# Transposes of quantised weights on the DMA queue, the causal mask of the second score pass on GpSimd, and new orders, in a pre-norm decoder layer

## The chip, the cores and the metric
The kernel runs on one core of one Trainium2 chip. The time is the device time of one execution in microseconds (us), the median of the runs shown. All engines run their own program in order and meet only at semaphores: TensorE (PE, with its weight loads PEld), VectorE (DVE), ScalarE (ACT), GpSimd (POOL) and SyncE (SP), which issues nearly all DMAs.

## The reference
Eight sequences of 128 tokens, 256 features, all float32. Three residual blocks follow one another, each fed by a layer norm without weights:

```
q, k, v = x@Wq+bq, x@Wk+bk, x@Wv+bv      # 16 query heads and 4 key heads of 16 features, with rotary embedding
scores  = sum over the 4 query heads of each key head of q.k / sqrt(16), causal mask, softmax, times v
x = x + attention @ Wo + bo
x = x + cross attention of norm(x) over ctx (keys = values = ctx, masked by mask_BxS2_bk0)
x = x + ffn(norm(x)):  w1 (1408x256), w2 (256x704), x and h each quantised to 127 steps per row
        h = silu(gate) * up,  gate and up are the two halves of x_q @ w1_q^T;  out = h_q @ w2_q^T
```

The einsum of the scores sums over the query heads of a group, so the kernel sums Wq over them first. Quantised values are whole numbers from -127 to 127 times one scale per row of the weight.

## The kernel before, in words
The host only lays the inputs out. Everything is loaded into SBUF at the start by SP, in the order of use: first weights, x, context, w1 in three parts, w2, the context again. One sequence (batch j, 0 to 7) fills the 128 partitions with its tokens. The work of a batch is a chain of small steps, and the chains of the eight batches are interleaved by lists of calls written out for each engine (PE from L560, ACT from L759, DVE from L1050, POOL from L1203). A step stands at its place in its engine's list and waits there for its semaphores, so what stands behind a late step is late too.

The steps of a batch:
- Self attention. project (PE) gives q, k and v; rotate (DVE), rotate_c (POOL) and rotate_sum (DVE) apply the rotary table; transpose_qk (PE) and evacuate_qk (ACT) give q and k by feature. The scores are computed twice. First pass: mask_scores writes the causal mask (-1e30) into PSUM with a matmul of the identity, scores adds q.k, and max_scores (DVE) takes each query's maximum. It goes into a spare column of q; transpose_q_max (PE) and evacuate_q_max (ACT) transpose that. Second pass, with keys on the partitions: mask_keys writes the transposed mask causal_T (4 matmuls a batch, L339), score_keys adds k.q minus the maximum, exp_self (ACT, L625) gives the probabilities p_self_T, 128 keys by 4 heads by 128 queries, already transposed. weigh_values (PE, L364, L367) multiplies them with v and with ones, for the sums. invert_sums, normalise_y (DVE), project_out (PE), residual_1 (DVE).
- Cross attention. square_1 (ACT) and rstd_2 (POOL, L1149, L1151) give the norm's scale; transpose_x1, cross_scores, max_cross, bias_cross, exp_cross, transpose_cross_p, readout (PE), residual_2 (DVE). The context is centred by centre_ctx (POOL) with means from mean_ctx (PE, L290: 16 products of 60 equal columns each, a matmul instruction twice for float32; one column is used).
- Feed forward. amax_x, step_x, invert_x (DVE), quantise_x (ACT), transpose_x_int (PE), evacuate_x_int (ACT); gate_product and up_product (PE, L456), where the gate weights are split in two parts, gate_hi (rounded by the write as float32r) and gate_lo (the rest); tanh_gate and finish_gate, or silu_gate; widen_gate (POOL, L1169) multiplies the gate by the row of up scales; hidden (DVE, L1021), amax_h, quantise_h, transpose_h, evacuate_h, down (PE, L538), scale_down (DVE), add_residual (POOL). Two buffers each hold the gate and the hidden values, so hidden(1) has to be done before up_product(2). The last batch is split in halves to shorten its chain.

Weights of the feed forward: amax_w1, scale_w1, invert_w1 (DVE) and quantise_w1 (ACT) give w1_int, int16, with output features on the partitions. They have to be transposed:
- gate: rescale_gate (POOL, L1157) multiplies by the scale, transpose_gate (PE, L408) transposes in float32 four blocks at a time into bank ps_r, upper_gate (ACT) and lower_gate (DVE, L951) take the two parts out of it;
- up: transpose_up (PE, L419) transposes whole numbers as 16-bit patterns, evacuate_up (ACT) converts; spread_up_scale (PE, L429) spreads the scales over the partitions, evacuate_up_scale (ACT) copies them to up_row;
- w2: transpose_w2 (PE, L439, and L441 for the scale), evacuate_w2 (DVE).

Filler matmuls (keep_warm, L263) stand where TensorE would wait at the start. GpSimd also makes the masks and zeroes buffers at the start, and rstd_1 (L1108) computes the first norm's scales, the last six batches in one call.

Of the kernel before, what the change touches and what calls it, by code (L numbers as in the profile page):

```python
# [32 lines left out]
def decoder_layer(nc, w_first_in, x_zero_in, x_first_in, x_second_in, wo_in, mask_in, x_in, xT_in, ctxT_in, ctx_in, w1_in, w2_in, out):  # L33
    P, B, DC, T = ctxT_in.shape
    D = DC * P
    H = N_KV
# [12 lines left out]
    GT = -(-FF // P)  # L49
    CM = 61  # L50
# [6 lines left out]
    with ExitStack() as stack:  # L57
# [7 lines left out]
        causal_T = sb("causal_T", [P, T], BF16)  # L65
# [28 lines left out]
        w1_q = sb("w1_q", [P, GT, D])  # L94
# [3 lines left out]
        up_row = sb("up_row", [P, FF])  # L98
# [4 lines left out]
        w2_int = sb("w2_int", [P, DC, FF], I16)  # L103
        w2_T = sb("w2_T", [P, FC, D], BF16)
# [61 lines left out]

        def x_token(j):
            return x_second[:, 0:D] if j == 1 else x_aug[:, j, 0:D]

        def x_feature(j, c):  # L170
# [16 lines left out]
            warm_ready causal_T_zero causal_T_ready wq_summed w_mean_done wqkv_c_ready bias_half_summed bias_summed bias_copied b_cos_done b_sin_done b_rope_ready  # L187
# [5 lines left out]
            scores_done negmax_done q_max_transposed q_max_T_ready keys_done p_T_ready  # L193
# [6 lines left out]
            w1_amax_done w1_scale_done w1_inv_ready w1_int_ready w1_q_ready w1_transposed gate_hi_ready gate_lo_ready  # L200
            up_transposed up_int_ready up_scale_spread up_row_ready
            w2_amax_done w2_scale_done w2_inv_ready w2_int_ready w2_transposed w2_ready
# [32 lines left out]
        def _(sp):  # L235
# [20 lines left out]
        def _(pe):  # L256
# [3 lines left out]
            def keep_warm(n):  # L260

                for _ in range(n):
                    nc.tensor.matmul(ps_r[:, 0:2 * T], warm[:, 0:P], warm[:, :], start=True, stop=True)  # L263
# [17 lines left out]
            def mean_ctx(last, k):  # L281
# [6 lines left out]
                for j in range(B):  # L288
# [47 lines left out]
            def mask_keys(j, heads):  # L336

                for h in heads:
                    nc.tensor.matmul(ps_s[:, h, 0:T], ident_b[:, :], causal_T[:, :], start=True, stop=False)  # L339

            def mask_other_keys(j):
                if j == 0:
                    done(pe, "causal_T_ready", 0)
                done(pe, "negmax_done", j)
                mask_keys(j, range(1, H))

            def score_keys(j):

                done(pe, "q_max_T_ready", j)
                mask_keys(j, range(1))  # L350
                for h in range(H):
                    nc.tensor.matmul(ps_s[:, h, 0:T], qk_T[j % 3][h * HP:(h + 1) * HP, 1, :],  # L352
                                     q_max_T[j % 3][h * HP:(h + 1) * HP, :], start=False, stop=True).then_inc(s["keys_done"], 1)

            def weigh_values(j):
# [6 lines left out]
                done(pe, "p_T_ready", j)  # L362
# [38 lines left out]
            def transpose_gate(p, last, k):  # L401
                bank_r_free(pe, last, k)
                if p == 0:
                    done(pe, "ident_ready", 0)
                done(pe, "w1_q_ready", p)
                for i in range(2):
                    for c in range(DC):
                        last = nc.tensor.transpose(ps_r[:, (2 * i + c) * P:(2 * i + c + 1) * P],  # L408
                                                   w1_q[:, 2 * p + i, c * P:(c + 1) * P], ident[:, :])
                last.then_inc(s["w1_transposed"], 1)  # L410

            def transpose_up(p, last, k):
# [859 lines left out]
```

## Time and profile before

| | us |
|---|---|
| median of 3 runs | 101.81 (101.38 to 102.7) |
| profiled execution | 102.22 |
| its span, first to last instruction | 100.4 |
| TensorE busy | 92.1 (92%) |
| VectorE busy | 75.4 (75%) |
| ScalarE busy | 65.1 (65%) |
| GpSimd busy | 61.5 (61%) |
| mean granted TensorE clock | 0.988 |

Busy times overlap; the shares are of the span. In the profile the matmul time of TensorE overlaps that of its neighbours, since matmuls are pipelined: the mean duration of one matmul is longer than what it adds. The chain of waits shows what each adds. A float32 matmul shows as two instructions. A clock of 1.00 is 2.4 GHz, 0.5 is 1.2 GHz.

### The profile page before, as it was taken

The page shows a single profiled execution, that of the slowest core. Times are in us where ns is not written, and L with a number is a line of the kernel's source. Part 1 is how long each engine was busy: PE and PEld are TensorE (multiplying, and loading weights), DVE is VectorE, ACT ScalarE, POOL GpSimd, SP SyncE. Part 2 cuts the span into 40 slices and gives each one's busy share as a digit, 9 for nine tenths or more (in the row PEclk, how much of TensorE's full clock was granted, in tenths as well). Part 3 has the DMA queues.
Part 4 walks back from the last instruction along what each step waited for, and adds up shares of the span by engine and source line. Part 5 has one row for each costly group of instructions (what it writes and reads, how often), then busy time and mean ns, then how long its engine had stood idle before and what let it go on. Part 6 is the DMA issues. An engine that isn't in the chain of part 4 may idle for free.

```text
span 100.4 us, 2487 instructions
## 1 busy us (share of the span) xinstructions
PE 92.1 (92%) x834; PEld 71.3 (71%) x834; DVE 75.4 (75%) x217; ACT 65.1 (65%) x175; POOL 61.5 (61%) x130
## 2 busy tenths in 40 slices
PE   5999699989999999999999999998999999999560
PEld 4788479766867787867877797776887977775220
DVE  5135979828999998697696669797878696998731
ACT  1403210489978677777787879689777897988420
POOL 5476666179922755976188674882489992872220
PEclk9999999999999999999999999999999999999995
DMA  2999999930000000000000000000000010021121
GB/s 35 368 342 421 416 407 415 351 98 3 0 7 3 0 3 0 7 0 0 7 0 0 0 0 7 3 0 0 0 0 0 7 52 3 0 104 52 52 104 52
DMA packets 4521, 8.34 MB, mean 83 GB/s; under 512 B 349, under 2 KB 3358, under 8 KB 4382
## 3 DMA queue, kind: packets, MB, share of 16 engines
q1 hardware_dynamic: 4272, 7.96, 21.6%
q10 hardware_dynamic: 238, 0.23, 0.7%
q8 instruction: 6, 0.10, 0.5%
q14 instruction: 5, 0.04, 0.1%
HBM read 7.15 MB, written 1.05 MB: 82 GB/s over the span
## 4 chain that ended last, share of the span: by engine, by line
PE 72%; DVE 13%; POOL 6%; issue 3%; ACT 3%; DVEq 0%; ACTq 0%; POOLq 0%
PE ps_s L456 11%; PE ps_r L263 8%; PE ps_q L304 6%; PE ps_y L538 4%; PE ps_r L290 4%; PE ps_y L372 3%; POOL gate_up L1169 3%; PE ps_r L399 3%; PE ps_s L352 3%; PE ps_s L328 3%; PE ps_x L388 2%; PE ps_q L312 2%; PE ps_y L364 2%; PE ps_s L339 2%; PE ps_s L482 2%
## 5 line engine op out<-in xcount | busy, mean ns | idle before, releaser
L1169 POOL TENSOR_TENSOR gate_up<-gate,up_row 128x704 f32<-128x704 f32 x7 | 11.9, 1699 | 6.6 <-ACT gate L738 5.0
L263 PE MATMUL ps_r<-warm 128*128 128x256 bf16 x58 | 9.5, 330 | 1.0 <-DVE warm L786 1.0
L1144 POOL TENSOR_TENSOR rot_c<-rot,b_rope 128x128 f32<-128x128 f32 x8 | 3.6, 456 | 9.1 <-DVE rot L861 9.1
L263 PEld LDWEIGHTS ps_r<-warm 128*128 128x128 bf16 x58 | 6.7, 120 | 3.1 <-DVE warm L786 1.0
L456 PE MATMUL ps_s<-gate_hi,x_int_T 128*128 128x352 f32 x28 | 7.7, 355 | 0.0
L884 DVE RECIPROCAL y_rsum<-ps_y 128x128 f32<-128x128 f32 x8 | 7.6, 950 | 0.1
L1200 POOL TENSOR_TENSOR y_out<-ffn,x_aug 128x256 f32<-128x256 f32 x7 | 4.8, 690 | 4.4 <-DVE ffn L1040 4.4
L538 PE MATMUL ps_y<-w_T,h_T 128*128 128x256 bf16 (+1 forms) x42 | 6.5, 275 | 0.9 <-DVE ffn L1040 0.8
L456 PE MATMUL ps_s<-up_int,x_int_T 128*128 128x352 f32 x32 | 6.8, 335 | 0.1
L456 PE MATMUL ps_s<-gate_lo,x_int_T 128*128 128x352 f32 x28 | 6.8, 323 | 0.0
L749 ACT ACTIVATE h_int<-hid,h_inv 128x704 int16<-128x704 f32 x7 | 6.1, 877 | 0.3 <-DVE h_inv L1035 0.3
L1026 DVE TENSOR_REDUCE h_amax<-hid 128x1 f32<-128x704 f32 x7 | 6.1, 877 | 0.1
L861 DVE TENSOR_TENSOR rot<-ps_q,rope_r 128x256 f32<-128x256 f32 x8 | 3.4, 422 | 3.7 <-PE ps_q L304 3.6
L620 ACT COPY q_max_T<-ps_s 128x128 f32<-128x128 f32 x8 | 2.1, 265 | 6.2 <-PE ps_s L334 5.9
L1021 DVE SCALAR_TENSOR_TENSOR hid<-ps_s,x_scale,gate_up 128x704 f32<-128x704 f32 x5 | 4.8, 951 | 1.8 <-PE ps_s L456 1.2
L538 PEld LDWEIGHTS ps_y<-w_T,h_T 128*128 128x128 bf16 (+1 forms) x42 | 3.6, 97 | 3.3 <-issue 1.5
L738 ACT ACTIVATE gate<-ps_s,x_scale 128x704 f32<-128x704 f32 x5 | 4.2, 847 | 2.3 <-PE ps_s L456 2.3
L879 DVE TENSOR_REDUCE qk_rot<-ps_s 128x4 f32<-128x512 f32 x8 | 5.5, 685 | 0.3
L304 PE MATMUL ps_q<-wqkv_c,xT 128*128 128x192 f32 x24 | 5.3, 341 | 0.5 <-ACT qk_T L614 0.5
L625 ACT ACTIVATE p_self_T<-ps_s 128x512 f32<-128x512 f32 x8 | 4.8, 596 | 1.4 <-PE ps_s L352 1.3
L1175 POOL TENSOR_SCALAR ctx_aug<-ctx_aug,valid_mean,ctx_negmean 128x256 f32<-128x256 f32 x8 | 4.4, 549 | 1.7 <-DVE ctx_negmean L853 1.7
L456 PEld LDWEIGHTS ps_s<-up_int,x_int_T 128*128 128x128 f32 x32 | 5.2, 189 | 0.2 <-DVE hid L1021 0.2
(197 smaller groups left out, 290.6 us busy)
## 6 DMA issues: line engine op xcount, KB each, us to landing
ctxT<-in_ctxT SPq DMA_DIRECT2D x1, 1024.0 KB, 8.7
w_raw<-in_w SPq DMA_DIRECT2D x2, 512.0 KB, 11.2
ctx_aug<-in_ctx SPq DMA_DIRECT2D x1, 1024.0 KB, 17.1
out_x<-y_out SPq DMA_DIRECT2D x8, 128.0 KB, 1.7
x_aug<-in_x SPq DMA_DIRECT2D x1, 768.0 KB, 7.0
xT<-in_xT SPq DMA_DIRECT2D x1, 768.0 KB, 9.9
w_raw<-in_w SPq DMA_DIRECT2D x1, 704.0 KB, 14.8
x_first<-in_x_first SPq DMA_DIRECT2D x1, 416.0 KB, 4.5
```

The lines of the kernel that those rows point to most:

```text
L263: nc.tensor.matmul(ps_r[:, 0:2 * T], warm[:, 0:P], warm[:, :], start=True, stop=True)
L304: last = nc.tensor.matmul(ps_q[:, 0:6 * QK], x_feature(j, c), wqkv_c[:, c, :, :], start=c == 0, stop=c == DC - 1)
L456: last = nc.tensor.matmul(ps_s[:, first + i, 0:FH], x_int_T[:, j, c, :], w[:, c, i * FH:(i + 1) * FH], start=c == 0 and w is parts[0], sto ...
L538: last = nc.tensor.matmul(ps_y[:, 0:D], h_T[j % 2][0:n, f, :], w2_T[0:n, f, :], start=f == 0, stop=f == FC - 1)
L625: nc.scalar.activation(p_self_T[j % 3][:, :, :], ps_s[:, :, 0:T], ACT.Exp).then_inc(s["p_T_ready"], 1)
L749: nc.scalar.mul(h_int[j % 2][:, :], hid[j % 2][:, :, :].rearrange("p i f -> p (i f)"), h_inv[:, j:j + 1]).then_inc(s["h_int_ready"], 1)
L879: nc.vector.tensor_reduce(qk_rot[j % 3][:, 0, :, DH], ps_s[:, :, 0:T], AX.X, ALU.max, negate=True).then_inc(s["negmax_done"], 1)
L884: nc.vector.reciprocal(y_rsum[j % 3][:, :], ps_ys).then_inc(s["y_rsum_done"], 1)
L1021: nc.vector.scalar_tensor_tensor(hid[j % 2][:, :, :], ps_s[:, 2:4, 0:FH], scale, gate_up[j % 2][:, :, :], ALU.mult, ALU.mult).then_inc(s[" ...
L1026: nc.vector.tensor_reduce(h_amax[:, j:j + 1], hid[j % 2][:, :, :].rearrange("p i f -> p (i f)"), AX.X, ALU.max, apply_absolute_value=True) ...
L1169: nc.gpsimd.tensor_tensor(gate_up[j % 2][:, :, :], gate[j % 2][:, :, :], up_row[:, :].rearrange("p (i f) -> p i f", i=2), ALU.mult).then_i ...
L1200: nc.gpsimd.tensor_tensor(y_out[:, j, :], ffn[j % 3][:, :], x_aug[:, j, 0:D], ALU.add).then_inc(s["y_out_ready"], 1)
```

## The change
- The second mask on TensorE (causal_T, mask_keys, mask_other_keys) is gone. score_keys starts its PSUM groups itself, exp_self exponentiates later keys too, and a new GpSimd step, drop_later_keys, sets those probabilities to 0 before weigh_values.
- w1_int is transposed by two DMA transposes on SP's queue into w1_T, with gate's 6 row blocks first, then up's 5. The scales of w1 are stored to DRAM element by element and loaded back as a row on every partition, w1_row, of which up_row is a part. Both reuse the memory of w1_raw.
- scale_gate (GpSimd) converts w1_T to float32 and multiplies with the row; upper_gate and lower_gate work on 704 columns per half, from SBUF. evacuate_up (ACT) reads w1_T.
- w2_int is converted to bf16 by widen_w2 (GpSimd), transposed by two more DMA transposes; its scale goes through DRAM as well.
- TensorE loses transpose_gate, transpose_up, spread_up_scale, transpose_w2 and the 7 fillers after scores(0). mean_ctx uses 8 columns instead of 60 and is split; its second half stands behind scores(1). mask_scores(0) moves behind transpose_qk(0).
- All four lists have new orders.

```diff
+            done(sp, "w1_scale_done", len(W1_PARTS) - 1)
+            sp.dma_start(w1_row_dram.rearrange("(o p) -> p o", p=P), w1_scale[:, :], allow_slow_non_contiguous=True).then_inc(s["w1_row_stored"], 16)
+            done(sp, "w1_int_ready", 2)
+            sp.dma_start_transpose(w1_T[:, 0:GT + 1, :, :].rearrange("p o c t -> p (o c) t"),
+                                   w1_int[:, 0:GT + 1, :].rearrange("p o d -> p (o d)")).then_inc(s["gate_T_loaded"], 16)
+            done(sp, "w1_int_ready", 4)
+            sp.dma_start_transpose(w1_T[:, GT + 1:WT, :, :].rearrange("p o c t -> p (o c) t"),
+                                   w1_int[:, GT + 1:WT, :].rearrange("p o d -> p (o d)")).then_inc(s["up_T_loaded"], 16)
+            sp.wait_ge(s["w1_row_stored"], 16)
+            sp.dma_start(w1_row[:, :], w1_row_dram.unsqueeze(0).to_broadcast([P, 2 * FF])).then_inc(s["w1_row_loaded"], 16)
+            done(sp, "w2_scale_done", 0)
+            sp.dma_start(w2_row_dram.rearrange("(c p) -> p c", p=P), w2_scale[:, :], allow_slow_non_contiguous=True).then_inc(s["w2_row_stored"], 16)
+            sp.wait_ge(s["w2_row_stored"], 16)
+            sp.dma_start(w2_row[:, :], w2_row_dram.unsqueeze(0).to_broadcast([P, D])).then_inc(s["w2_row_loaded"], 16)
+            for c in range(DC):
+                done(sp, "w2_bf_ready", c)
+                sp.dma_start_transpose(w2_T[:, :, c * P:(c + 1) * P], w2_bf[:, c, :]).then_inc(s[f"w2_T_{c}_loaded"], 16)
...
             def score_keys(j):
                 done(pe, "q_max_T_ready", j)
-                mask_keys(j, range(1))
                 for h in range(H):
                     nc.tensor.matmul(ps_s[:, h, 0:T], qk_T[j % 3][h * HP:(h + 1) * HP, 1, :],
-                                     q_max_T[j % 3][h * HP:(h + 1) * HP, :], start=False, stop=True).then_inc(s["keys_done"], 1)
+                                     q_max_T[j % 3][h * HP:(h + 1) * HP, :], start=True, stop=True).then_inc(s["keys_done"], 1)
...
+            def upper_gate(c):
+                done(act, "gate_T_ready", c)
+                nc.scalar.copy(gate_hi[:, c, :], gate_T[:, c, :]).then_inc(s["gate_hi_ready"], 1)
+            def evacuate_up(c):
+                act.wait_ge(s["gate_T_loaded"], 16)
+                act.wait_ge(s["up_T_loaded"], 16)
+                nc.scalar.copy(up_int[:, c, 0:FL], w1_T[:, GT, c, FL:P])
+                nc.scalar.copy(up_int[:, c, FL:FF].rearrange("p (o t) -> p o t", t=P), w1_T[:, GT + 1:WT, c, :]).then_inc(s["up_int_ready"], 1)
...
+            def lower_gate(c):
+                done(dve, "gate_T_ready", c)
+                done(dve, "gate_hi_ready", c)
+                nc.vector.tensor_tensor(gate_lo[:, c, :], gate_T[:, c, :], gate_hi[:, c, :].bitcast(F32), ALU.subtract).then_inc(s["gate_lo_ready"], 1)
...
+            def drop_later_keys(j):
+                done(pool, "p_T_ready", j)
+                nc.gpsimd.affine_select(out=p_self_T[j % 3][:, :, :], in_=p_self_T[j % 3][:, :, :], compare_op=ALU.is_ge, fill=0.0, base=0,
+                                        pattern=[[0, H], [1, T]], channel_multiplier=-1).then_inc(s["p_causal_ready"], 1)
+            def scale_gate(c):
+                done(pool, "w1_int_ready", 4)
+                pool.wait_ge(s["gate_T_loaded"], 16)
+                pool.wait_ge(s["w1_row_loaded"], 16)
+                nc.gpsimd.tensor_copy(gate_T[:, c, 0:GT * P].rearrange("p (o t) -> p o t", t=P), w1_T[:, 0:GT, c, :])
+                nc.gpsimd.tensor_copy(gate_T[:, c, GT * P:FF], w1_T[:, GT, c, 0:FL]).then_inc(s["gate_T_widened"], 1)
+                done(pool, "gate_T_widened", c)
+                nc.gpsimd.tensor_tensor(gate_T[:, c, :], gate_T[:, c, :], w1_row[:, 0:FF], ALU.mult).then_inc(s["gate_T_ready"], 1)
+            def widen_w2(c):
+                done(pool, "w2_int_ready", c)
+                if c == 0:
+                    done(pool, "w2_bf_zero", 0)
+                nc.gpsimd.tensor_copy(w2_bf[:, c, 0:FF], w2_int[:, c, :]).then_inc(s["w2_bf_ready"], 1)
...
 # GpSimd's list
+            rstd_1(0, 1, 1); scale_rope(0); sum_bias(); rope_bias(); rotate_c(0); rstd_1(1, 2, 2); centre_x(0)
+            scale_rope(1); rotate_c(1); centre_x(1); rstd_1(2, B, 3); drop_later_keys(0); scale_rope(2)
+            centre_x(2); centre_x(3); scale_rope(3); rotate_c(2); centre_x(4); centre_x(5); scale_rope(4)
+            centre_x(6); scale_rope(5); centre_x(7); centre_ctx(0); drop_later_keys(1); scale_rope(6)
+            rotate_c(3); rstd_2(0); centre_ctx(1); widen_w2(0); centre_ctx(2); drop_later_keys(2); rotate_c(4)
+            scale_gate(0); rstd_2(1); drop_later_keys(3); centre_ctx(3); rotate_c(5); rstd_2(2); scale_gate(1)
+            drop_later_keys(4); scale_rope(7); rotate_c(6); centre_ctx(4); whole_x2(0); rstd_2(3); centre_ctx(5)
+            scale_x(0); drop_later_keys(5); whole_x2(1); rotate_c(7); widen_w2(1); rstd_2(4); centre_ctx(6)
+            drop_later_keys(6); scale_x(1); whole_x2(2); centre_ctx(7); rstd_2(5); drop_later_keys(7)
+            whole_x2(3); scale_x(2); whole_x2(4); rstd_2(6); widen_gate(0); scale_x(3); whole_x2(5); rstd_2(7)
+            scale_x(4); widen_gate(1); whole_x2(6); scale_x(5); widen_gate(2); widen_gate(3); scale_x(6)
...
 # ScalarE's list, its part around the new waits
+            quantise_w1(3); evacuate_q_max(1); evacuate_qk(2); exp_self(1); square_1(0); quantise_w1(4)
+            evacuate_x1(0); scale_v(3); quantise_w2(0); evacuate_q_max(2); evacuate_qk(3); exp_cross(0)
+            exp_self(2); evacuate_cross_p(0); evacuate_up(0); quantise_w2(1); scale_v(4); evacuate_x1(1)
+            evacuate_up(1); evacuate_q_max(3); evacuate_qk(4); square_1(1); exp_self(3); upper_gate(0)
...
 # VectorE's list, its part around the w1 scales
+            rotate_sum(1); amax_w1(0); scale_w1(0); invert_w1(0); amax_w1(1); scale_w1(1); invert_w1(1)
+            rotate(2); invert_sums(0); max_scores(1); normalise_y(0); rotate_sum(2)
+            amax_w1(2); scale_w1(2); invert_w1(2); keep_valid(); residual_1(0); negate_ctx_mean(); rotate(3)
...
 # TensorE's list, its parts around the first batches and the last cross attention
+            keep_warm(11, ps_x); transpose_qk(0); mask_scores(0); project(1); scores(0); mean_ctx(None, 0)
+            transpose_q_max(0); transpose_qk(1); score_keys(0); project(2); mask_scores(1); weigh_values(0)
+            scores(1); mean_ctx_half(1); transpose_q_max(1); project_out(0); transpose_qk(2); score_keys(1)
...
+            gate_product(2); transpose_cross_p(7); readout(7, "x2_ready", 6); up_product(1)
+            transpose_x_int(4, "x2_ready", 7); gate_product(3); transpose_x_int(5, "x_int_T_ready", 4)
+            up_product(2); transpose_h(0); gate_product(4); down(0); transpose_h(1)
```

## Rows read from the trace of the kernel before

**Rows 1.** Windows: stretch, its length, busy us (instructions) of PE, PEld, DVE, ACT, POOL; clock; DMA share; GB/s.

```profile
25.00:30.00 5.00, 4.62 (x56) 3.60 (x56) 4.64 (x10) 4.26 (x13) 3.12 (x8) 1.00 0.02 3
30.00:35.00 5.00, 4.97 (x59) 3.84 (x60) 4.69 (x15) 3.76 (x12) 2.56 (x6) 1.00 0.00 2
...
50.00:55.00 5.00, 5.00 (x65) 3.86 (x63) 3.67 (x11) 3.83 (x13) 4.08 (x12) 1.00 0.00 0
```

**Rows 2.** Chain of waits in order of time: start us, us, engine, tile, line.

```profile
66.04 1.67 POOL gate_up L1169
...
68.94 0.91 DVE hid L1021
...
91.96 0.57 DVE hid L993
```

**Rows 3.** Chain of waits, TensorE's pieces that the change touches and their neighbours.

```profile
7.29 0.39 PE ps_x L273 x4
...
14.01 0.87 PE ps_r L263 x7
...
15.20 3.71 PE ps_r L290 x32
...
21.80 0.45 PE ps_r L408 x4
...
34.76 0.17 PE ps_s L339 x3
...
48.98 0.67 PE ps_r L429 x6
...
57.09 0.45 PE ps_r L419 x6
...
70.80 0.47 PE ps_r L439 x6
71.27 0.42 PE ps_r L441 x2
```

**Rows 4.** Groups by line and form, VectorE: busy us, mean ns, idle before.

```profile
L951 DVE TENSOR_TENSOR gate_lo<-ps_r,gate_hi 128x256 fp32r<-128x256 f32 x5 | 1.9, 417 | 0.6 <-ACT gate_hi L666 0.6
L986 DVE TENSOR_TENSOR gate_up<-gate,up_row 128x352 f32<-128x352 f32 x2 | 1.4, 749 | 0.0
```

**Rows 5.** GpSimd: one window (POOL is the fifth busy time), its start, three groups.

```profile
17.60:67.70 50.10, 48.68 (x529) 38.04 (x529) 40.57 (x111) 38.85 (x121) 32.76 (x73) 1.00 0.08 24
16.22 1.34 POOL L1108 TENSOR_TENSOR r<-ln_var,pow_exp 128x6 f32<-128x6 f32 x1
L1157 POOL TENSOR_SCALAR w_q<-w_int,w_scale 128x256 f32<-128x256 int16 x6 | 2.8, 483 | 2.7 <-ACT w_int L657 2.7
L1149 POOL TENSOR_SCALAR ln_var<-x_sumsq 128x1 f32<-128x1 f32 x8 | 1.5, 191 | 1.4 <-ACT y_out L630 0.9
L1089 POOL TENSOR_SCALAR_AFFINE_SELECT causal<-causal 128x128 bf16<-128x128 bf16 x1 | 0.3, 292 | 0.1
```

**Rows 6.** Chain of waits, batch 3: its second scores, its weigh_values.

```profile
40.56 0.43 PE ps_s L352 x8
...
43.85 0.40 PE ps_y L364 x8
```

**Rows 7.** DMA: a queue with packets, MB, share; issues with KB, us to landing.

```profile
q10 hardware_dynamic: 238, 0.23, 0.7%
...
ctx_aug<-in_ctx SPq DMA_DIRECT2D x1, 1024.0 KB, 17.1
out_x<-y_out SPq DMA_DIRECT2D x8, 128.0 KB, 1.7
...
w_first<-in_w_first SPq DMA_DIRECT2D x1, 384.0 KB, 3.7
```

**Rows 8.** Window from hid(1) to the last hidden, columns as in rows 1.

```profile
68.90:92.00 23.10, 22.82 (x163) 17.56 (x161) 19.47 (x49) 19.19 (x38) 14.96 (x20) 1.00 0.07 24
```

**Rows 9.** Window at the end of the span, columns as in rows 1.

```profile
98.00:100.40 2.40, 0.00 (x0) 0.00 (x0) 0.34 (x1) 0.00 (x0) 0.00 (x0) 0.51 0.16 55
```

More of the change, by code:

```diff
@@ L287, in mean_ctx, with mean_ctx_half @@
                 pe.wait_ge(s["ctxT_loaded"], 16)
-                for j in range(B):
+                mean_ctx_half(0)
+            def mean_ctx_half(half):
+                means = ps_r[:, 0:B * CM].rearrange("p (b n) -> p b n", n=CM)
+                for j in range(half * B // 2, (half + 1) * B // 2):
                     for c in range(DC):
@@ L586, in _ @@
-            up_product(1); readout(6, "x_int_T_ready", 4); transpose_cross_p(7); up_product(2)
-            transpose_w2(0, "x2_ready", 6); gate_product(3); transpose_w2(1, "w2_ready", 0); transpose_h(0)
-            gate_product(4); up_product(3); transpose_x_int(5, "w2_ready", 1); down(0); transpose_h(1)
-            readout(7, "x_int_T_ready", 5); gate_product(5); up_product(4); transpose_x_int(6, "x2_ready", 7)
-            down(1); transpose_h(2); gate_product(6); up_product(5); down(2); transpose_h(3)
@@ new lines, in _ @@
+            scores(1); mean_ctx_half(1); transpose_q_max(1); project_out(0); transpose_qk(2); score_keys(1)
+            project(3); transpose_x1(0); mask_scores(2); scores(2); weigh_values(1); cross_scores(0)
+            transpose_q_max(2); transpose_qk(3); score_keys(2); project(4); transpose_cross_p(0); project_out(1)
+            readout(0, "valid_ready", 0); mask_scores(3); transpose_x1(1); scores(3); weigh_values(2)
+            transpose_qk(4); transpose_q_max(3); cross_scores(1); score_keys(3); project(5); project_out(2)
@@ new lines, in _ @@
+            mask_scores(4); scores(4); transpose_cross_p(1); weigh_values(3); transpose_q_max(4)
+            readout(1, "x2_ready", 0); transpose_x1(2); transpose_qk(5); score_keys(4); cross_scores(2)
+            project(6); mask_scores(5); project_out(3); scores(5); transpose_cross_p(2)
+            transpose_x_int(0, "x2_ready", 1); weigh_values(4); transpose_x1(3); transpose_q_max(5)
+            readout(2, "x_int_T_ready", 0); cross_scores(3); transpose_qk(6); score_keys(5); project(7)
+            project_out(4); transpose_x_int(1, "x2_ready", 2); mask_scores(6); transpose_cross_p(3); scores(6)
@@ new lines, in _ @@
+            transpose_x1(4); weigh_values(5); transpose_q_max(6); readout(3, "x_int_T_ready", 1); score_keys(6)
+            cross_scores(4); transpose_qk(7); mask_scores(7); project_out(5); scores(7)
+            transpose_x_int(2, "x2_ready", 3); transpose_cross_p(4); weigh_values(6); transpose_q_max(7)
+            transpose_x1(5); readout(4, "x_int_T_ready", 2); score_keys(7); cross_scores(5); project_out(6)
+            gate_product(0); transpose_cross_p(5); weigh_values(7); transpose_x_int(3, "x2_ready", 4)
@@ new lines, in _ @@
+            transpose_x1(6); up_product(0); cross_scores(6); readout(5, "x_int_T_ready", 3); gate_product(1)
+            project_out(7); transpose_cross_p(6); transpose_x1(7); readout(6, "x2_ready", 5); cross_scores(7)
+            gate_product(2); transpose_cross_p(7); readout(7, "x2_ready", 6); up_product(1)
+            transpose_x_int(4, "x2_ready", 7); gate_product(3); transpose_x_int(5, "x_int_T_ready", 4)
+            up_product(2); transpose_h(0); gate_product(4); down(0); transpose_h(1)
@@ L596, in _ @@
+            transpose_x_int(6, "x_int_T_ready", 5); up_product(3); gate_product(5); up_product(4); down(1)
+            transpose_h(2); gate_product(6); up_product(5); transpose_x_int(7, "x_int_T_ready", 6)
+            transpose_h(3); down(2); up_product(6); last_gate(0); transpose_h(4); last_gate(1); down(3)
+            transpose_h(5); up_product(7); down(4); transpose_h(6); down(5); down(6); last_transpose_h_a()
+            last_transpose_h_b(); last_down_a(); last_down_b()
         @block.scalar
```

265 lines of the change are left out of this document (69 added, 196 removed).

## The prediction
> **What bounds the kernel now.** I read the windows of 5 us first [rows 1]. TensorE is busy 4.6 to 5.0 of every 5 us from 25 to 90 us, always at its upper clock (granted 1.00), and VectorE is close behind (4.6 to 4.7 of 5 between 25 and 35). So between 30 and 60 us TensorE's own work sets the pace. GpSimd has 0.9 to 2.4 us of idle in those 5. The chain of waits [rows 2] says the same with one exception: from 60 to 69 us it runs through GpSimd: the first two gate products times the scale row (L1169, 1.7 us each) with small pieces between, then VectorE's hid(1) at 68.94; the rows are the second L1169 and the two ends. From there TensorE again, to a tail from 91.96 in which one batch passes serially through all engines. Two places matter here: the end of the second L1169, 67.7 us (call it T), and the 32.7 us from T to the end of the span. The profiled execution took 102.2 us at a span of 100.4; the median is 101.8, so a span converts to a median by +1.4.
>
> **TensorE.** It loses the second causal mask, 32 matmuls at 0.17 per 3: 1.8 us; 3 groups of gate transposes at 0.45: 1.35; 2 of up transposes at 0.45: 0.9; 2 spreads of the up scale at 0.67: 1.34; the w2 groups, 2 x (0.47 + 0.42): 1.78; 7 filler matmuls: 0.87 [rows 3]. Sum 8.0 us, of which 1.8 lie behind T. The context means are cut from 60 columns to 8, but 32 matmuls of 60 columns take 0.116 us each while those of 64 columns take 0.098 and the f32 transposes of 128 columns 0.11 [rows 3]: the weights set that price, so I take 0 (bounds: 0, and 52/60 of 3.71, 3.2 us). Half of them are put behind the second scores. With the fillers gone, the first q_max transpose comes at about 15.9 instead of 18.9. That is latency, not work: it lets the first exp go earlier, and the half comes back.
>
> **VectorE and ScalarE.** VectorE loses five lower_gate pieces of 0.42 and one of 0.28 (2.4), and evacuate_w2, 1.9. It gains two subtractions of 704 columns with both operands in SBUF. The nearest rows are L986, 0.75 us for 352 columns, so 1.5 each at most, and L951, 0.42 for 256 with one operand in PSUM, so 1.1 [rows 4]. I take 1.3 each; net -1.7, and the bounds move it by 0.4. ScalarE's copies of gate, up and up scale go from 4.4 to about 3.8. Neither moves the end; the cover is that both have idle beside TensorE and GpSimd, and if it were gone they would cost nothing new, since both lose work.
>
> **GpSimd.** This is where the bill falls. Before, it is busy 32.76 us between 17.6 (its 6-batch pow ends, L1108) and T [rows 5]. Out: 6 rescales at 0.48, 2.8 us. In: 8 selects of 512 columns. The selects of 128 columns took 0.29; a one-input op of 1 column (L1149) takes 0.19 and one of 256 (L1157) 0.48 [rows 5], so 0.6 if most of 0.29 is overhead, 1.17 if none is; nearer to the first, since every one-input row shows overhead: 0.7, 5.6 us in sum. In: twice a copy of 640 and one of 64 columns (0.92 and 0.27 on the line through those two rows) and a product of 704, the shape of L1169, 1.7 [rows 2]: 5.8. In: two w2 copies of 704, 1.0 each: 2.0. And rstd_2(7) is now ahead of T: 0.74. That is 44.1 us of work, and about 30 dependent pairs with the 0.1 us that the chain shows as issue, 2.8. T can't be before 17.6 + 44.1 + 2.8 = 64.5 us. The new memset for w2 (0.6 to 1.4 by the other memsets) and the causal_T pair it replaces lie in GpSimd's idle before 5.4 us: 0.
>
> The GPSIMD Engine Reference of the Trainium skill (section 3.1) puts a two-input operation on GpSimd at about twice VectorE's time; here L1169 [rows 2] takes 1.7 against the 1.5 that 704 columns would be in two halves of L986 [rows 4], only 1.13 times. By the page the two products of scale_gate would rather be 3.0 each, an estimate, and T 2.6 later.
>
> The select also adds a link: exp, then select, then weigh_values. Before, TensorE ran 2 to 3 us of other work between the last score matmul and weigh_values (batch 3: 40.99 to 43.85 [rows 6]), and exp uses 0.8 of it. 0.8 more fits, if GpSimd comes to it in time. It is in order: behind a wait for a DMA, all selects are late, then TensorE.
>
> **The new DMA train on SP's queue.** Each step of it, in order: store of w1_scale (1408 single elements), transposes of gate and of up, row load of 704 KB to 128 partitions, then w2's. All SP loads were issued by 5.9 us, the last landed at 23, and SP's output stores start after 80, so nothing else is hurt. Start: VectorE's third amax_w1 is now behind max_scores(1), about 22.8 us. Prices [rows 7]: ACT's small-packet queue moved 238 packets in 0.7% of 16 engines x 100.4 us, 47 ns each, so 1408 packets over 16 engines are 4.1 us, and +1.4 for a landing (a 128 KB store lands in 1.7). Row load: 704 KB at 0.4 MB/us, 3.2. Transposes: no row shows one. Below, a plain 384 KB load, 3.7. Above, the slowest landing, 17.1. If each 128-element piece is a packet, gate has 1536 (4.5 us) and up 1280 (3.8). I take 2.5 us of queue time each, nearer to the plain load, since the bytes are the same. The store's packets are then through at 27, the transposes at 29.5 and 32, the row at 32 + 1.8 of data, and it lands at about 34.5. By packets alone (4.5 and 3.8) it is 39; by the lowest prices, with the store as quick as a 128 KB one, below 30.
>
> Waiters: scale_gate(0) on GpSimd, reached at 30.3 (12.3 us of work from 17.6, plus small waits), with rstd_2(1), drop_later_keys(3) and rotate_c(5) behind it; evacuate_up(0) on ScalarE behind evacuate_cross_p(0), about 29, with quantise_w2(1), scale_v(4) and q_max(3) behind it. The row at 34.5 is a wait of 4.2; I charge 3 us of it and T = 67.5, since GpSimd would have waited about 1 us for rotations anyway. w2's train needs its row and blocks only at down(0), after 75: 0.
>
> The DMA page of the Trainium skill (DMA: Bandwidth & Descriptors, Latency and other measured facts) gives 261 GB/s for a DMA transpose, which would be an estimate of 1.5 us for gate's 393 KB and would make the train some 3 us shorter. No row here can show it. Its rule that a non-contiguous last dim lowers to one descriptor per element (section Rules for kernel authors) is what the 1408 packets would be.
>
> **Behind T.** From 68.9 to 92.0 all engines have 19 to 23 us in 23 [rows 8]. TensorE leaves 1.78 (w2), and gate_product(3) 1.53, readout(7) 0.63 and one x_int transpose 0.13 now stand ahead: 4.1. VectorE leaves 2.0 of w2 and about 1.7 of two residuals with their maxima. ScalarE has 19.2 and drops under 1, so it is next: the stretch becomes about 19. Gain 4. The tail from the last hidden is the same work: 8.4 us.
>
> **Sum.** 100.4 + (67.5 - 67.7) - 4 = 96.2 of span, +1.4: 97.6 us.
>
> **Rivals.**
>
> A. The train is in time (transposes near the plain load): T falls to GpSimd's 64.5, a span of 93.2, 94.6 us; a little more if selects cost 0.6. TensorE agrees: up_product(1) ends at 68.7 before, less 6.3 removed, plus 1.2 moved ahead, 63.6. For: all queues are empty then. Against: two engines arrive at their waits around 30.
>
> B. The train goes at packet prices: row at 39, a stall of 8.7, T = 73.2: 103.3; 102 where GpSimd's other waits absorb part. For: the 47 ns rest on small packets as these are. Against: they are from plain loads. No difference that can be measured (2% is 2.0 us, what a measurement of this kernel tells from no change).
>
> C. Slower. The transposes take as long as the slowest load or longer, one after the other. Break-even: T + 32.7 - 4 + 1.4 = 101.8 gives T = 71.7, a stall of 7.2, the row at 37.5. Two transposes at 17.1 and the row land at 27 + 17 + 17 + 3 = 64: T = 98, 128 us. At 8 each it is about 46, T = 80, 110 us. It decides from 40 us on for the row: 104 us. For: the trace has landings of 10 to 17 us. Against: those stood in a full queue, and this one is empty.
>
> D. The clock. With fillers gone and TensorE waiting near 30 us, the granted clock could fall to 1.2 GHz. The trace shows a mean of 0.51 in the last 2.4 us, in which TensorE has no matmul [rows 9], and 1.00 in all stretches before the tail. 3 to 6 us of TensorE work at half the clock add 3 to 5 us to the forecast: 101 to 103. "TensorE: Matmul & The Clock Gate" of the Trainium skill (Part 1) says that idleness brings the throttle; the row agrees in kind.
>
> **Chances.** Forecast (95.5 to 99.8) 0.38; A 0.20; B 0.18; C 0.18; D 0.06. Faster by over 2% (below 99.8): forecast and A, 0.58, less 0.01 for its upper edge. Within 2%: most of B and D, 0.22. Slower: C and B's edge, 0.21. Range: 93.5 (A with cheap selects) to 103.5 (B's end), with C and a little of A left out, about 2 in 10.
>
> **What would show it.** Right: SP's transposes land 3 to 5 us after issue, GpSimd idle of 2 to 5 us ahead of gate_T's first copy, selects at 0.7, the second L1169 ending at 66 to 69, TensorE about 84 busy, hid(1) to the last hidden 19. Wrong: transposes over 8 us (C), no wait at gate_T (A), a PEclk below 9 around 30 us (D), or selects over 1 us, which add 3 us to T.

## The result and the profile after

The changed kernel takes 106.19 us (median of 4 runs, 105.43 to 106.27) against 102.25 of the kernel before on the same chip: ratio 1.040 (95% interval 1.029 to 1.050), slower. The forecast was 97.6 with a range to 103.5, so it was wrong in sign and in size. The profiled execution took 106.22 us at a span of 104.4. Here and below, ratios and intervals compare only each kernel's fast runs, those within 1.5% of its quickest, while a median with its spread is of all runs, and where a single run is fast no interval stands.

The windows answer to [rows 1]; columns as there:

```profile
15.00:20.00 5.00, 4.86 (x47) 3.81 (x49) 4.09 (x12) 3.33 (x9) 3.81 (x8) 0.66 1.03 384
...
30.00:35.00 5.00, 3.28 (x39) 2.18 (x37) 3.13 (x10) 0.84 (x3) 1.28 (x3) 1.00 1.29 42
35.00:40.00 5.00, 1.56 (x8) 1.53 (x8) 0.93 (x4) 3.48 (x10) 0.51 (x1) 0.67 0.64 185
40.00:45.00 5.00, 5.00 (x45) 3.65 (x44) 1.86 (x5) 3.22 (x11) 4.58 (x9) 0.65 0.04 2
```

Between 30 and 40 us, where TensorE used to be full, it has 4.8 us of work in 10, and then it is full at a clock of 0.65. The waits from 24 to 46 us (who waited <- for whom: sum, times, longest) name the releaser:

```profile
POOL w_raw L1101 <- DMA w_raw<-w_row_dram: 7.7, 1, 7.7
ACT up_int L637 <- DMA w_T<-w_int: 5.4, 1, 5.4
PEld ps_q L339 <- issue: 5.4, 1, 5.4
PE ps_q L339 <- ACT v_pad L576: 5.2, 1, 5.2
```

GpSimd stands at scale_gate(0) for the row, ScalarE at evacuate_up(0) for the transpose of up, and TensorE waits for the scale_v that stands behind that in ScalarE's list. The row lands at about 39.4 us. From 39.5 to the end of the second gate_up product GpSimd then never waits longer than 0.2 us, so the row sets that end. The DMA issues (KB, us to landing) answer to [rows 7]:

```profile
w_raw<-w_row_dram SPq DMA_DIRECT2D x1, 704.0 KB, 4.6
...
w_T<-w_int SPq DMA_TRANSPOSE x2, 10.7
w_row_dram<-w_scale SPq DMA_DIRECT2D x1, 5.5 KB, 11.1
w_row_dram<-w_scale SPq DMA_DIRECT2D x1, 1.0 KB, 10.4
```

The smallest transfers are the slowest: 5.5 KB in 11.1 us, 1 KB in 10.4. The point T, the end of the second gate_up product, and VectorE's hid(1) and last hidden answer to [rows 2] (timeline: start, us, engine, line):

```profile
73.31 1.69 POOL L1122 TENSOR_TENSOR gate_up<-gate,w_raw 128x704 f32<-128x704 f32 x1
75.69 0.94 DVE L960 SCALAR_TENSOR_TENSOR hid<-ps_s,x_square,gate_up 128x704 f32<-128x704 f32 x1
...
95.91 0.57 DVE L932 SCALAR_TENSOR_TENSOR hid<-ps_s,x_scale,gate_up 128x352 f32<-128x352 f32 x1
```

T is 75.0 instead of 67.7. From T to the end it is 29.4 us, before 32.7. So all of the loss, and more, stands ahead of T: 7.3 us later, and 3.3 of them back behind it.

### The profile page after: what moved, and what is told of

Same layout as the page of the kernel before. It is cut to its first block, busy times and chain, and to the rows that moved or that the text cites. A ratio compares the mean times of both kernels' runs of the same rounds, so it can differ in the third digit from the quotient of the medians.

```text
span 104.4 us, 2307 instructions
## 1 busy us (share of the span) xinstructions
PE 89.2 (85%) x743; PEld 67.6 (65%) x743; DVE 73.6 (71%) x207; ACT 64.5 (62%) x172; POOL 72.7 (70%) x139
## 4 chain that ended last, share of the span: by engine, by line
PE 58%; ACT 10%; DMA 10%; DVE 8%; POOL 6%; issue 5%; DVEq 0%; ACTq 0%; POOLq 0%
PE ps_s L429 13%; DMA w_T<-w_int 10%; PE ps_r L285 7%; PE ps_q L331 5%; PE ps_r L317 4%; PE ps_s L367 3%; PE ps_y L511 3%; PE ps_x L403 3%; PE ps_y L387 2%; PE ps_s L355 2%; PE ps_y L379 2%; POOL ctx_aug L1128 2%; PE ps_q L478 2%; PE ps_q L339 1%; PE ps_x L478 1%
## 5 line engine op out<-in xcount | busy, mean ns | idle before, releaser
L1122 POOL TENSOR_TENSOR gate_up<-gate,w_raw 128x704 f32<-128x704 f32 x7 | 11.9, 1700 | 2.3 <-ACT gate L689 2.3
L339 PE MATMUL ps_q<-ident,qk_rot 128*128 128x128 f32 x16 | 3.4, 300 | 5.6 <-ACT v_pad L576 5.2
L285 PE MATMUL ps_r<-warm 128*128 128x256 bf16 x40 | 7.2, 356 | 1.1 <-DVE warm L737 1.1
L331 PE MATMUL ps_q<-wqkv_c,xT 128*128 128x192 f32 x24 | 7.6, 456 | 0.6 <-ACT qk_T L582 0.6
L285 PEld LDWEIGHTS ps_r<-warm 128*128 128x128 bf16 x40 | 5.0, 130 | 2.8 <-DVE warm L737 1.1
L1101 POOL CAST w_raw<-w_T 128x640 f32<-128x640 int16 x2 | 1.4, 719 | 7.7 <-DMA w_raw<-w_row_dram 7.7
L331 PEld LDWEIGHTS ps_q<-wqkv_c,xT 128*128 128x128 f32 x24 | 5.3, 257 | 1.6 <-ACT qk_T L582 1.1
L339 PEld LDWEIGHTS ps_q<-ident,qk_rot 128*128 128x128 f32 x16 | 2.0, 149 | 6.2 <-issue 5.4
L1086 POOL TENSOR_SCALAR_AFFINE_SELECT p_self_T<-p_self_T 128x512 f32<-128x512 f32 x8 | 5.1, 644 | 1.2 <-ACT p_self_T L593 0.8
L403 PE MATMUL ps_x<-ctxT,x1c_T 128*128 128x128 f32 x32 | 5.8, 308 | 0.0
```

Of the source, the lines that this page charges most:

```text
L285: nc.tensor.matmul(bank[:, 0:2 * T], warm[:, 0:P], warm[:, :], start=True, stop=True)
L331: last = nc.tensor.matmul(ps_q[:, 0:6 * QK], x_feature(j, c), wqkv_c[:, c, :, :], start=c == 0, stop=c == DC - 1)
L339: last = nc.tensor.transpose(ps_q[:, QT0 + i * T:QT0 + (i + 1) * T], qk_rot[j % 3][:, i], ident[:, :])
L403: last = nc.tensor.matmul(ps_c, x1c_T[j % 3][:, c, :], ctxT[:, j, c, :], start=False, stop=c == DC - 1)
L1086: nc.gpsimd.affine_select(out=p_self_T[j % 3][:, :, :], in_=p_self_T[j % 3][:, :, :], compare_op=ALU.is_ge, fill=0.0, base=0, pattern=[[0, ...
L1122: nc.gpsimd.tensor_tensor(gate_up[j % 2][:, :, :], gate[j % 2][:, :, :], up_row[:, :].rearrange("p (i f) -> p i f", i=2), ALU.mult).then_i ...
```

## The experiments

All ratios are to the kernel before, timed on the same chip; a difference between two variants is often one between two chips. An element store is one that writes every scale as a transfer of its own, 4 bytes long. The code cuts are shortened.

**e1_probe.** The whole train on the queue of the kernel before, one transfer after the other, results unused:

```diff
+ sp: store w1_scale by elements; wait; transpose gate; wait; transpose up; wait; load row; wait;
+     store w2_scale by elements; wait; store w1_scale, 64 bytes apart; wait; store it as 128 lines; wait
```

> The kernel before, with seven DMAs more on SP's queue between 28 us and the output stores, each issued only when the one before has landed, so each is alone: store of the w1 scales as 1408 single elements, transpose of gate's 6 row blocks, of up's 5, row load of 704 KB, store of the w2 scales as 256 single elements, a store of the w1 scales with 64 bytes between elements, and one in 128 runs of 44 bytes. Nothing uses their results. Theory S (the element stores are slow in themselves, the transposes quick): first store 9 us or more alone, w2's too, transposes at 5 us or less, time 102. Rival T (the transposes are slow and held the stores up, which shared the engines with them): first store 5.5 us, w2's under 3, transposes 8 to 10 us alone. Either way the time stays within 1% of before, since SP has nothing else to do.

Measured: 106.38 us, ratio 1.041 (1.033 to 1.049), though nothing waits for any of it. SP's own waits show what each costs alone:

```profile
SPq L258 <- DMA w_row_dram<-w_scale: 10.4, 1, 10.4
SPq L269 <- DMA w_row_dram<-w_scale: 7.2, 1, 7.2
SPq L271 <- DMA pad_dram<-w_scale: 3.4, 1, 3.4
SPq L267 <- DMA w_raw<-w_row_dram: 3.2, 1, 3.2
SPq L261 <- DMA w_raw<-w_int: 2.9, 1, 2.9
```

The element stores take 10.4 and 7.2 us in an empty queue; the same 1408 elements 64 bytes apart take 3.4 and gate's transpose 2.9 beyond its issue (3.9 from issue to landing, the median of both). So the transposes are quick and the store is slow by itself. That the time rose by 4 us was foreseen by no theory.

**e2_warm.** The changed kernel with the seven fillers after scores(0) and 60 columns in mean_ctx again.

```diff
- scores(0); mean_ctx(None, 0)        - CM = 9
+ scores(0); keep_warm(7); mean_ctx(None, 0)        + CM = 61
```

> The changed kernel with the 7 fillers behind scores(0) again and 60 columns in the context means. Theory (the early falls of the clock are off the path, since ScalarE and GpSimd wait for DMAs whose start hangs on VectorE): clock at 1.00 from 10 to 33 us, but TensorE then waits longer ahead of 38 us, the long idle and the second fall stay: 105 to 106.5. Rival (the early clock costs what it takes): 3 us less, 103.

Measured: 107.04, ratio 1.046 (1.037 to 1.055). No gain: the clock is at 1.00 from 15 to 35 us now, but the waits for the transfers take up what it gives (ScalarE stands 6.7 us for up's transpose instead of 5.4).

**e3_later.** The changed kernel with evacuate_up and upper_gate (ACT), lower_gate (DVE) and scale_gate (POOL) some steps later in their lists.

> The changed kernel with scale_gate, evacuate_up, upper_gate and lower_gate some batches later in the lists of GpSimd, ScalarE and VectorE, so that their DMAs have landed; nothing else. Theory (the wait of 5.2 us of TensorE and the 7.3 us at 1.2 GHz behind it are the loss): both go, 106.2 - 5.2 - 3.6 = 97.4, with 96.5 to 99.5 as GpSimd paces the second half. Rival (GpSimd's added work is the loss and the wait only hides it): 103 or more.

Measured: 104.61, ratio 1.024 (1.016 to 1.033). The two DMA waits are gone, but only 1.6 us of the 106.2 with them. The element stores are still there, and in the profiled execution, the longest of the four, GpSimd waits elsewhere, for a sum of squares of ScalarE that is late itself:

```profile
36.29 0.19 POOL L1092 TENSOR_SCALAR ln_var<-x_sumsq 128x1 f32<-128x1 f32 x1 [4.51 <-ACT y_out L598]
...
40.99 0.60 ACT L593 ACTIVATE p_self_T<-ps_s 128x512 f32<-128x512 f32 x1 [0.17 <-PE ps_s L367]
...
41.66 0.64 POOL L1086 TENSOR_SCALAR_AFFINE_SELECT p_self_T<-p_self_T 128x512 f32<-128x512 f32 x1 [2.06 <-issue]
```

The last idle is marked "issue", which reads as if nothing were waited for. It is a wait for data all the same: the select needs the probabilities of ScalarE's line above, which end at 41.59. So this run says only that the loss doesn't hang on those two waits alone.

**e4_select.** The select alone: the kernel before with the 32 mask matmuls replaced by 8 selects on GpSimd.

> The kernel before with the second mask's 32 matmuls replaced by the 8 selects on GpSimd, nothing else of the change. Theory: TensorE loses 1.8 us, GpSimd gains 8 x 0.64 = 5.1; the link of 0.7 us fits between exp and weigh_values: 100.5 to 102. Rival: the selects stand late in GpSimd's list and hold TensorE: 104.

Measured: 102.87, ratio 1.010 (1.006 to 1.014). TensorE is busy 90.5 us instead of 92.1 and idle for as much more: the work is gone, the time is not. Whether the link or the 5.1 us more on GpSimd costs it, no run separates.

**e5_store and e6_moves.** The kernel before with one part of the train each: w1's element store alone, or everything of w1 but with the scales stored as lines.

```diff
e5: + sp.dma_start(w1_row_dram "(o p) -> p o", w1_scale)        # 1408 elements
e6: + sp.dma_start(w1_row_dram "(p o) -> p o", w1_scale)        # 128 lines of 44 bytes
e6: + both transposes, row load
```

> The kernel before with one transfer more: SP's queue stores w1_scale (128 x 11) to a row in DRAM element by element, as the changed kernel does, once it is complete (about 24 us). Nothing waits for it. Theory H (the store of single 4-byte elements keeps the DMA engines busy for some 10 us, and the next block of each engine's instructions, which the same DMA engines bring, comes late; engines then stand still until the store is through): most of the 4.2 us that all seven transfers together cost comes back, 104.5 to 106.5, with an instruction packet of 2 to 3.5 us instead of 0.4, and two or three engines idle to the moment at which the store lands. Rival M (it is the volume: two transposes and the 704 KB row load compete with the kernel's work): the store alone costs nothing, 101.8 to 102.6.

> The kernel before with all the bulk transfers of w1 on SP's queue, their results unused: both transposes (gate and up), the 704 KB load of a row to all partitions, and the scale stored as 128 lines of 44 bytes in place of 1408 single elements. Theory H: 101.8 to 102.8, no engine waits for instructions. Rival M: 104.5 to 106.5, and e5 costs nothing.

Measured: e5 105.48 (102.95 to 107.66) beside 102.47 of the kernel before; e6 102.23, ratio 1.000 (0.996 to 1.005). 1.4 MB of transposes and row cost nothing, 5.5 KB in single elements 0.5 to 5 us. Late beside the store are the packets that bring the engines their own instructions; the DMA view counts them on the same 16 DMA engines. In the kernel before, such a packet around 24 us (window of 1 us; packets, MB, share of 16 engines):

```profile
q14 instruction: 1, 0.01, 3.6%
```

In e5, windows 25 to 26 and 27 to 28:

```profile
q14 instruction: 1, 0.01, 20.8%
...
q8 instruction: 1, 0.02, 17.7%
```

20.8% of 16 engines over 1 us is 3.3 us for one packet, where it was 0.6. It ends about 28.8, and there two engines go on, out of idles that no data explain:

```profile
28.77 0.37 ACT L672 CAST gate_hi<-ps_r 128x256 fp32r<-128x256 f32 x1 [1.13 <-remote]
28.81 0.42 DVE L865 TENSOR_TENSOR rot<-ps_q,rope_r 128x256 f32<-128x256 f32 x1 [0.56 <-remote]
```

The changed kernel has two of them, at 32 (1.9 us) and at 42 (2.9 us). But e1 shows that the packet can't be all of it. Its long packet, 3.4 us, is over at 33.1, and the longest idles end 4 us later, just before the store lands at 37.8:

```profile
37.44 0.96 DVE L911 RECIPROCAL y_rsum<-ps_y 128x128 f32<-128x128 f32 x1 [3.65 <-remote]
37.57 0.27 ACT L647 COPY q_max_T<-ps_s 128x128 f32<-128x128 f32 x1 [4.07 <-remote]
```

So the engines stand still while an element store is under way; by what they are held isn't shown.

**e7_line and e8_line_warm.** The changed kernel with both scale rows stored in lines of 512 bytes; e8 has e2's edit as well.

```diff
- sp.dma_start(w1_row_dram "(o p) -> p o", w1_scale)
+ pe:  transpose(ps_r[0:11, 384:512], w1_scale, ident)
+ act: copy(scale_line[0:11], ps_r[0:11, 384:512])
+ sp.dma_start(w1_row_dram "(o p) -> o p", scale_line[0:11])      # between the two transposes
  (w2's two columns in the same way)
```

> The changed kernel, with both scale rows stored as whole lines: TensorE transposes w1_scale (128 x 11) and w2_scale (128 x 2) into a free part of PSUM, ScalarE copies them out (one short copy each), and SP stores 11 (2) lines of 512 bytes; the rest as it was. Theory H: store in 1.5 us, transposes landed by 32, row by 33; the 5.4 us wait of ScalarE and the 7.7 us wait of GpSimd shrink to under 2 together; the second gate_up product ends near 69 instead of 75.0; 99 to 101.5. Rival M: the transposes stay near 10 us, 104 or more. Rival C (the clock falls at 16 and 23 us, and what it takes from the attention stages sets the end once the waits are gone): the waits go, the second product ends at 71 to 73, 101.5 to 104.

> The kernel of e7 and with it what e2 put back: seven 256-column fillers after the first scores and 60 columns in place of 8 in each product of the mean of ctx. Theory H alone: as e7 within 0.5. Rival C: 1 to 3 us less than e7, with a granted clock of 1.00 to the end of the attention stages, and perhaps less than the kernel before.

Measured: e7 99.72, ratio 0.977 (0.971 to 0.982); e8 99.60, ratio 0.973 (0.966 to 0.981). Both beat the kernel before. e7's transfers:

```profile
w_raw<-w_row_dram SPq DMA_DIRECT2D x1, 704.0 KB, 4.3
...
w_T<-w_int SPq DMA_TRANSPOSE x2, 3.8
```

The same transposes land in 3.8 us instead of 10.7, GpSimd's wait for the row is 1.2 instead of 7.7, ScalarE's for up's transpose is gone, and T is 68.4:

```profile
66.70 1.68 POOL L1143 TENSOR_TENSOR gate_up<-gate,w_raw 128x704 f32<-128x704 f32 x1
```

**e9_store3 and e10_padded3.** The kernel before with three stores of the same 1408 elements in turn, to neighbouring places or 64 bytes apart.

> The kernel before with the element store of e5 three times, one after the other (each waits for the one ahead), from 24 us on; nothing else waits for them. It doubles and trebles the suspected cost: e5 alone ran from 102.95 to 107.66. Theory H (blocks of instructions come late while such a store is under way): the stores hold the DMA engines for about 31 us, three or four blocks fall into that, 106 to 114 and less spread relative to the cost. Rival M (the four microseconds of e5 are chance, or belong to the clock): 102 to 104.

> As e9, three stores of the same 1408 elements of 4 bytes, but each element to a place of its own 64 bytes from the next. The number of packets and of bytes is that of e9. Theory H with neighbours as the cause of the slow store: 3.8 us each, no instruction packet much over 1 us, 102 to 103.5. Rival N (the number of small packets is what delays instructions, wherever they go): as e9 in proportion to the time that the stores take, a third of its excess or more, 104 to 106.

Measured: e9 112.28 (106.91 to 113.5); e10 102.36, ratio 1.002 (0.997 to 1.007). With as many packets and bytes, only the neighbours cost: 10 us by the median and 4.7 in the quickest run, against nothing. Four instruction packets take 3.4, 2.8, 3.2 and 3.9 us in e9; in e10 none takes over 1.2.

**e11_line_warm_masks.** e8 with the select undone: the mask by 32 matmuls again.

> The kernel of e8 with the select undone: the causal mask of the second score pass added on TensorE by 32 matmuls as in the kernel before, the 8 selects of GpSimd gone. In e8 GpSimd is busy 4.4 to 4.8 of each 5 us from 35 to 60 us. Theory G (GpSimd sets the time of the attention stages there, its 8 selects of 0.65 us with it): 97 to 99. Rival P (TensorE takes back 3.5 us of mask matmuls and is the bound again): 100 to 102. Neither: 99.2 to 100.

Measured: 98.62 (98.12 to 98.97), ratio 0.965 (0.959 to 0.971), the quickest of all. The select is worth minus 1.0 us here (e8 and e11 ran on different chips, and their intervals overlap), minus 0.7 in e4.

**e12, e13, e15, e16.** One of the two rows stored by elements again, in e7 (e12, e13) and in e8 (e15, e16).

> The kernel of e7 with one thing back as in the changed kernel: the 256 scales of w2 are stored element by element. Theory H: the store takes 7 to 10 us from about 33 us and w2's transposes follow late, which nothing waits for; an instruction block that falls into it comes late: 100.5 to 103, w1's store being the larger part of the change's loss. Rival (256 elements are too few to matter): 99.4 to 100.2.

> The kernel of e7 with w1's 1408 scales stored element by element as in the changed kernel, and w2's 256 as lines. Counterpart of e12. Theory H (each element store costs by what needs the DMA engines while it runs; w1's runs over both w1 transposes and an instruction block): up transpose landed at 35 to 37, ScalarE waits 4 to 6 us for it, GpSimd 6 to 8 us for the row; 103 to 106, near the changed kernel. Rival (w2's store, which alone gave about 4 us in e12, is most of it): 99.5 to 102.

> The kernel of e8 (rows stored as lines, fillers and wide mean products kept; 99.6) with w1's 1408 scales stored by elements. Theory H: up transpose and row late as in the changed kernel, granted clock 1.00 to 30 us: 103 to 105.5. Rival C (most of e13's loss was the low clock): 100 to 102.

> The kernel of e8 with w2's 256 scales stored by elements. If the loss of e12 was mostly the low clock (its profile is 2.5 us late before that store starts, and its quickest run took 99.86): 99.5 to 101, with one instruction packet near 2.5 us. Rival H2 (it is the store): 102.5 to 104.5.

Measured: w2's row by elements 103.71 (99.86 to 104.55) in e12 and 99.92, ratio 0.977 (0.970 to 0.984), in e16; w1's 105.09, ratio 1.024 (1.019 to 1.030), in e13 and 105.67, ratio 1.031 (1.022 to 1.040), in e15. Only the pair on e8 is clean: in the profiles of e12 and e13 TensorE has the clock of 0.50 to 0.57 from 15 to 25 us, ahead of what the edit touches. By it w1's store costs 6.1 us and w2's 0.3; the median of e12 taken alone would have put 4 us on w2's store, while its quickest run, 99.86, agrees with e16.

**e14, e17, e18.** The clock: e11 without fillers and with 8 columns (e14), the kernel before with the same two cuts (e17), e11 with the fillers but 8 columns (e18).

> The kernel of e11 without what e2 put back: no fillers after the first scores, and 8 columns in place of 60 in the mean of ctx. Theory W (the low clock at 15 to 30 us lies where the kernel waits for the row and its loads anyway): granted clock 0.5 to 0.85 there as in e7, and a time within 0.6 us of e11's 98.6. Rival C (TensorE is the bound, so each microsecond at 1.2 GHz is paid): 100 to 102.

> The kernel before, without the seven fillers between the first scores and the mean of ctx, and with 8 columns in place of 60 in its 16 products: the change's cut of cheap TensorE work, alone. Theory C2 (TensorE falls to 1.2 GHz for some 5 to 13 us from 16 us on and is the bound there): 1 to 5 us slower, 103 to 107. Rival W (as in the pair e7 and e8, nothing): 101.5 to 102.7.

> The kernel of e11 (98.6) with its seven fillers kept and 8 columns in each mean product: between e11 and e14 (102.6). If the fillers hold the clock: 98.4 to 99.4. If the wide mean products do: 101 to 103.

Measured: e14 102.56 (100.63 to 103.58), ratio 0.988 (0.983 to 0.993), against e11's 98.62 and 0.965; e17 104.96, ratio 1.028 (1.021 to 1.035); e18 99.26, ratio 0.972 (0.964 to 0.980; three runs within 0.04 us, one at 102.74). In e17's windows the clock stands at half while TensorE is counted busy, and the 32 matmuls of mean_ctx take 5.67 us where 32 of 60 columns took 3.71 [rows 3]:

```profile
15.00:20.00 5.00, 4.96 (x25) 4.53 (x24) 3.80 (x9) 0.52 (x2) 2.20 (x4) 0.50 1.04 382
20.00:25.00 5.00, 4.54 (x27) 3.54 (x30) 0.98 (x4) 2.76 (x8) 2.69 (x6) 0.50 0.18 58
```

```profile
13.46 5.67 PE L290 MATMUL ps_r<-mean_w,ctxT 128*128 128x8 f32 x32
```

and in e11's it is at full:

```profile
15.00:20.00 5.00, 5.00 (x63) 3.94 (x63) 3.81 (x8) 2.99 (x8) 4.39 (x9) 1.00 1.04 385
20.00:25.00 5.00, 5.00 (x55) 4.26 (x58) 4.09 (x13) 4.01 (x13) 3.06 (x7) 1.00 0.76 147
```

The cheap work held the clock, the seven fillers most of it: without the wide columns alone (e18) the ratio goes from 0.965 to 0.972, without the fillers too (e14) to 0.988. Without both the kernel before loses 2.6 us, and e11 2.4 by the ratios, 3.9 by the medians. In e7 and in the changed kernel nothing is lost that can be measured; I put that down to the waits for the row and for GpSimd, which cover it there, and no run tests that cover alone.

## Why the prediction was wrong

- **The step that failed is the price of the store.** It took 47 ns a packet from small packets of a plain load [rows 7], 4.1 us and 1.4 to land. The store landed after 11.1 us and takes 10.4 alone. That it is the neighbouring places and not the number of packets is shown by e10. No case of the prediction had a dearer store: its early end made the store as quick as one of 128 KB, and its late end, the row at 39, raised only the transposes.
- **"Nothing else is hurt" failed with it.** What is late beside the store: the transposes that were issued 0.5 and 2.5 us behind it (10.7 us instead of 3.8), and the blocks of instructions (1.7 to 3.9 us instead of 0.3 to 1.4), which no part of the prediction looked at. Taking the element stores out moves e2 to e8, 107.0 to 99.6: 7.4 us. e15 gives 6.1 of them to w1's row and e16 0.3 to w2's; the last 1.0 comes only with both, or is the difference of two chips. "w2's train: 0" was right to a few tenths in e16, by cover and not by speed.
- **What it did to T.** The prediction charged 3 us of waiting for the row and 2.8 of other idle on GpSimd. From 17.6 to T the changed kernel has 7.7 and 6.2, and 43.5 us of work where 44.1 were predicted: 4.7 + 3.4 - 0.6 us more, T at 75.0 instead of 67.5.

```profile
17.60:75.00 57.40, 49.49 (x463) 37.34 (x461) 41.67 (x114) 39.71 (x121) 43.48 (x86) 0.89 0.43 57
```

With T 7.3 us later than before and 3.3 us gained behind it the span is 104.4. The step from span to time is 1.8 us in both profiled executions; the prediction had 1.4, since it set a median against the span of one execution.
- **The transposes** were priced at 2.5 us of queue time each; they land in 3.6 to 4.1 us (the median of w1's two) where no element store is about (e1, e6, e7, e8, e11, e14, e18), so the sign "3 to 5 us after issue" holds for them. Rivals B and C both have a train that comes late, for the wrong reason: they blamed the transposes. B even has its time, the row at 39 for the measured 39.4, and that is luck, since dear transposes stand there for the dear store. C's sign, transposes over 8 us, came true in the changed kernel and pointed at the wrong transfer. The Trainium skill (DMA: Bandwidth & Descriptors, Latency and other measured facts) would give gate's transpose 1.5 us, an estimate from its 261 GB/s; the trace has 2.9 beyond the issue and bears the longer price out.
- **GpSimd's work** was right. e7 shows it without the store; the busy time (fifth) from 17.6 to its T is 43.3 us, predicted 44.1, and T is 68.4, predicted 67.5. That T is so near is in part luck: the wait for the row is 1.2 us instead of the 3 that were charged, and the other idle 6.3 instead of 2.8.

```profile
17.60:68.40 50.80, 47.81 (x465) 35.67 (x463) 40.77 (x113) 39.64 (x123) 43.32 (x86) 0.93 0.25 64
```

The select takes 0.64 (predicted 0.7), the product of 704 columns 1.67 (1.7), a w2 copy 0.77 (1.0), and VectorE's lower_gate 0.94 (1.3); the lines are the changed kernel's:

```profile
L1086 POOL TENSOR_SCALAR_AFFINE_SELECT p_self_T<-p_self_T 128x512 f32<-128x512 f32 x8 | 5.1, 644 | 1.2 <-ACT p_self_T L593 0.8
...
L901 DVE TENSOR_TENSOR gate_lo<-w_raw,gate_hi 128x704 fp32r<-128x704 f32 x2 | 1.9, 939 | 0.0
```

The GPSIMD Engine Reference of the Trainium skill (section 3.1) puts two-input work on GpSimd at about twice VectorE's time. The trace has 1.67 against 0.94 us for the like shape on VectorE, 1.8 times, so the factor is near. The 3.0 us that the prediction made of it was too long, since it started from VectorE's 1.5 for two halves.
- **TensorE's work** was right too: the prediction has about 84 us, and e8, nearly always at the upper clock, has 85.4 with 0.9 of fillers. The changed kernel's 89.2 have the time at the lower clock in them.
- **The select's link** was costed as fitting into TensorE's other work. e4 and e11 say that the select loses 0.7 to 1.0 us where it was to gain TensorE 1.8; whether by the link or by its work on GpSimd is open.
- **Behind T** the gain was 4; it is 3.3, since from hid(1) to the last hidden it is 20.2 us instead of 19 [rows 8].
- **The clock** had a chance of 6 in 100 (rival D), 0 was taken for the columns, and the fillers were counted as 0.87 us gained. The 0 is right as a duration at the upper clock: in the changed kernel the first half of 8-column products takes 1.95 us, 0.12 each. Both are wrong as a consequence: e17, without fillers and wide columns, loses 2.6 us, most of it by the fillers if e18 is a guide. The rival expected the fall while TensorE waits near 30 us. It does fall then, at 36.7 us, when TensorE has done nothing since 33.3, but first at 16 us, while TensorE is busy.

So with rows stored as lines the forecast's mechanism stands and its size is 2 us off: 99.7 against 97.6. What the sign hung on was the way in which 5.5 KB are stored.

## What to carry to other kernels

Price a transfer by its pieces and where they land, not by its bytes: a transposed store of single elements is worth a small transpose on TensorE and one copy to turn it into lines. A slow transfer that nothing waits for can still cost: look for instruction packets that take microseconds, and for idles that end with no releaser, and check each such idle against the end of what it reads before you believe it. Fillers and wide columns that look free may be what holds the clock, so take them out one at a time, and last.

## What the runs showed of the hardware

- 1408 stores of 4 bytes to neighbouring places in DRAM take 10.4 us beyond their issue, 256 take 7.2, 1408 to places 64 bytes apart 3.4 (2.9 and 3.9 in e10), 128 lines of 44 bytes 1.4 from issue to landing (in e1). The Trainium skill (DMA: Bandwidth & Descriptors, Specifications) says that transfers under 512 bytes become a read, a change and a write. All these pieces are under that size, and those 64 bytes apart cost other work nothing (e10), so it is the shared neighbourhood that is dear. How the hardware orders them isn't shown.
- One packet of instructions takes 0.3 to 1.4 us in the kernel before and up to 3.9 beside such a store. That engines wait for the late packet fits the times at which it ends and they resume in e5, and not in e1; no run takes it away alone. In e16 such a packet of 2.3 us goes with a loss of 0.3.
- TensorE's clock falls to 1.2 GHz while it is counted busy 4.96 of 5 us (e17), so busy time alone does not tell whether the clock holds.
- Open: why e14's runs spread by 3 us when e11's don't. Their profiles differ in how long the low clock lasts.
